# A decoder chain on one Trainium2 core: the norm after cross attention begun earlier, and its turn put inside the matmuls ahead of it

## The reference

```python
# layer 0 (decoder block), after its causal self attention
x = x + cross_attention(ln2(x), ctx) @ out_w + out_b          # 16 heads of 16
x = x + gelu(ln3(x) @ mlp1_w + mlp1_b) @ mlp2_w + mlp2_b
# layer 1: routing attention over the context, gates u and r, candidate, layernorm
# layer 2, after its self attention
x = x + cross_attention(ln2(x), ctx) @ ca_wo + ca_bo          # 16 heads of 64
a, g = split(ln3(x) @ ff_w1 + ff_b1)
x = x + (a * gelu(g)) @ ff_w2 + ff_b2
# layer 3
x = layernorm(cross_attention8(x, ctx) @ Wo + x) * gamma + beta
```

## Time and profile before

| | |
|---|---|
| median of 3 runs | 2139.35 us (2139.18 to 2140.95) |
| profiled execution, its own time | 2139.63 us |
| its span | 2137.7 us, so 1.9 us lie around it |
| PE busy | 2017.7 us (94%) |
| DVE, ACT, POOL busy | 1127.9, 937.1, 749.0 us |
| mean granted PE clock | 0.981 of full |

### The profile page before, as it was taken

How to read it: one execution, slowest core, us unless ns; L and a number is a source line. 1 busy time by engine, 2 the same in 40 slices (tenths; PEclk the granted TensorE clock), 3 DMA queues, 4 the chain that set the end, 5 groups by cost and what they waited for, 6 DMA issues and landing times. The chain is left out here.

```text
span 2137.7 us, 26706 instructions
## 1 busy us (share of the span) xinstructions
PE 2017.7 (94%) x10334; PEld 1200.1 (56%) x10334; DVE 1127.9 (53%) x2009; ACT 937.1 (44%) x1449; POOL 749.0 (35%) x563
## 2 busy tenths in 40 slices
PE   5989998899998999999999999999999999999997
PEld 3544444677676854444544445444543868677776
DVE  4677772534545357756555555555454243546453
ACT  3356666333434425554355554555356431222221
POOL 1222212021212126657566664666464010212121
PEclk9999999999999979999999999999999999999999
DMA  7734332000000021100000000000000430000000
GB/s 147 137 36 52 43 57 85 1 1 1 1 1 1 1 67 39 32 1 1 1 1 1 1 1 1 1 1 1 1 1 1 113 97 1 1 11 3 7 10 10
DMA packets 48044, 51.81 MB, mean 24 GB/s; under 512 B 14682, under 2 KB 38940, under 8 KB 47620
## 3 DMA queue, kind: packets, MB, share of 16 engines
q1 hardware_dynamic: 47924, 50.19, 11.3%
HBM read 41.24 MB, written 8.80 MB: 23 GB/s over the span
## 5 line engine op out<-in xcount | busy, mean ns | idle before, releaser
L1992 POOL TENSOR_TENSOR total<-total,pr 128x1024 f32<-128x1024 f32 x183 | 444.4, 2428 | 232.4 <-ACT pr L2202 215.6
L2202 ACT ACTIVATE pr<-sc 128x1024 f32<-128x1024 f32 x256 | 260.1, 1023 | 266.6 <-PE sc L1868 262.1
L2013 DVE TENSOR_REDUCE pmax<-ring 128x1 f32<-128x512 f32 x512 | 314.5, 684 | 98.2 <-PE ring L1816 98.2
L1868 PE MATMUL sc<-q_full,k_full 64*128 64x512 f32 x1024 | 295.0, 589 | 0.0
L1886 PE MATMUL o<-pr,v_pair 128*64 128x512 f32 x1024 | 247.7, 605 | 0.0
L1816 PE MATMUL ring<-k_round,q_round 64*128 64x512 f32 x512 | 214.2, 569 | 5.8 <-DVE k_round L2007 2.0
L645 ACT ACTIVATE probs<-s 128x512 f32<-128x512 f32 (+1 forms) x304 | 154.8, 579 | 95.7 <-PE s L360 94.9
L483 DVE TENSOR_REDUCE row_max<-s 128x1 f32<-128x1024 f32 (+3 forms) x128 | 125.0, 1019 | 59.2 <-PE s L346 58.9
L1816 PEld LDWEIGHTS ring<-k_round,q_round 64*128 64x128 f32 x512 | 78.7, 190 | 137.3 <-DVE pmax L2013 115.2
L1868 PEld LDWEIGHTS sc<-q_full,k_full 64*128 64x128 f32 x1024 | 129.0, 191 | 26.1 <-issue 16.8
L1886 PEld LDWEIGHTS o<-pr,v_pair 128*64 128x64 f32 x1024 | 62.2, 136 | 138.7 <-issue 121.6
(11 more groups left out here) (362 smaller groups left out, 3438.5 us busy)
## 6 DMA issues: line engine op xcount, KB each, us to landing
qk_dram<-qk_parts SPq DMA_DIRECT2D x32, 192.0 KB, 2.7
q_stack<-qk_dram SPq DMA_DIRECT2D x48, 128.0 KB
k_stack<-qk_dram SPq DMA_DIRECT2D x48, 128.0 KB
x<-in_x SPq DMA_DIRECT2D x4, 512.0 KB, 7.4
region<-in_L_xattn_mlp_w SPq DMA_DIRECT2D x2, 1024.0 KB, 7.9
region<-in_L_xattn_ff_w SPq DMA_DIRECT2D x1, 2048.0 KB, 18.8
out<-region SPq DMA_DIRECT2D x8, 256.0 KB, 2.2
region<-in_L_xattn_sa_wo SPq DMA_DIRECT2D x1, 1024.0 KB, 8.0
```

The lines of the kernel that those rows point to most:

```text
L1868: ins = te.matmul(s2[at % 2][:, j], kf[n % 2][head[j], keys], qf[n % 2][head[j], halves[half]], start=False, stop=True)
L1992: pool.tensor_tensor(out=total[half][:], in0=other[:], in1=probs[at % KEPT][:], op=ALU.add).then_inc(sums, 1)
L2013: dve.tensor_reduce(part_max[:, j, t, half:half + 1], ring[bank_of_max(i)][:], AX.X, ALU.max).then_inc(s1_free, 1)
L2202: act.activation(probs[here % KEPT][:], s2[at % 2][:], ACT.Exp).then_inc(s2_free, 1)
```

## The change

In the first chain, DVE's order in `cross` is written anew: stream 0's add, statistics and moments come between stream 1's reciprocals and stream 1's multiply `vT`; stream 0's normalise comes behind that multiply; then stream 1 follows. PE does the turn of stream 0's norm between the two tiles of stream 1's projection, where it was behind both. In the second chain, PE does the turn of stream 0's norm between chunks 4 and 5 of the eight in stream 1's last values. And in the last block of the second chain DVE finishes stream 0 altogether (norm, scaling) before it adds stream 1's last result.

```diff
-def cross_tensor(te, ch, e, name, i, vw, cols, out_bias):
+def cross_tensor(te, ch, e, name, i, vw, cols, out_bias, between=None):
...
         for c in range(cols // P):
+            if between is not None and s + t == 2 and c == cols // P // 2:
+                between()
...
                         ins = add_bias(te, ch, dst, 0)
+                        if s == 1 and t == 0:
+                            turn_step(te, ch, e, i, "n3", 0)
                     ins.then_inc(ch.te[s].sem, ch.te[s].one("ca.out"))
...
                 cross(i, first)
-                turn_step(te, ch, e, i, "n3", 0)
...
+                def moments(s):
+                    add_vector(dve, ch, e, "ca.x", i, "ca.out", s, bank=1, x=own(s, i))
+                    norm_vector(dve, ch, "n3", i, lambda s: own(s, i), lambda s: after_spare(dve, ch, s, "ca.x", i),
+                                scaled=True, streams=[s])
...
+                inverse(0)
+                divided(0)
+                inverse(1)
+                moments(0)
+                divided(1)
+                normed(0)
+                moments(1)
+                normed(1)
...
                 cross(i)
-                for s in range(B):
-                    add_vector(dve, ch, e, "ca.x", i, "ca.out", s, bank=1, x=own(s, i))
-                    norm_vector(dve, ch, "n3", i, x, lambda s: after_spare(dve, ch, s, "ca.x", i), streams=[s])
...
-                cross_tensor(te, ch, e, "cb", i, e.vw2, 1024, 0)
-                turn_step(te, ch, e, i, "n9", 0)
+                cross_tensor(te, ch, e, "cb", i, e.vw2, 1024, 0, lambda: turn_step(te, ch, e, i, "n9", 0))
...
                         tail.dve[s].sem, tail.dve[s].one("x.last"))
-                if last:
-                    finish_block(i, True)
+                    if last:
+                        finish_block(i, True, [s])
```

More of the change, by code:

```diff
@@ L771, in norm_gpsimd, with scaled_vector @@
             ch.pool[s].sem, ch.pool[s].one(f"{name}.rstd"))
-def scaled_vector(dve, ch, name, i, source, gain, bias, dst, done):
-    for s in range(B):
+def scaled_vector(dve, ch, name, i, source, gain, bias, dst, done, streams=range(B)):
+    for s in streams:
         after(dve, ch.pool[s], f"{name}.rstd", i)
@@ L1388, in cross, with inverse @@
                                           op=ALU.subtract).then_inc(*one(s, f"less{t}"))
-                for s in range(B):
+                def inverse(s):
                     after(dve, ch.act[s], "ca.exp1", i)
@@ L1395, in cross, with divided @@
                     dve.reciprocal(ch.total[s][:], ch.total[s][:]).then_inc(*one(s, "inverse"))
+                def divided(s):
                     after(dve, ch.act[s], "ca.raw", i)
@@ L1399, in cross, with normed @@
                                       in1=caT[s][:].rearrange("p g t -> p (g t)"), op=ALU.mult).then_inc(*one(s, "vT"))
+                def moments(s):
+                    add_vector(dve, ch, e, "ca.x", i, "ca.out", s, bank=1, x=own(s, i))
+                    norm_vector(dve, ch, "n3", i, lambda s: own(s, i), lambda s: after_spare(dve, ch, s, "ca.x", i),
+                                scaled=True, streams=[s])
+                def normed(s):
+                    after(dve, ch.pool[s], "n3.rstd", i)
+                    for t in range(2):
+                        ins = dve.tensor_scalar(ch.h[s][:, t, :], own(s, i)[:, t, :], ch.moments[s][:, t, 0:1],
+                                                ch.rstd[s][:, t:t + 1], ALU.subtract, ALU.mult)
+                    ins.then_inc(ch.dve[s].sem, ch.dve[s].one("n3.h"))
+                inverse(0)
[6 more added lines that the diff above has]
+                normed(1)
             def finish_block(i):
@@ L2582, in head, with finish_block @@
                     ins.then_inc(*one("h", s))
-            def finish_block(i, waits):
+            def finish_block(i, waits, streams=range(B)):
                 last = lambda s: ch.xc[s][:]
-                norm_vector(dve, tail, "n10", i, last, lambda s: after_spare(dve, tail, s, "x.last", i), scaled=True)
+                norm_vector(dve, tail, "n10", i, last, lambda s: after_spare(dve, tail, s, "x.last", i), scaled=True,
+                            streams=streams)
                 if waits:
-                    for s in range(B):
+                    for s in streams:
                         dve.wait_ge(stored[s], 16 * i)
-                scaled_vector(dve, tail, "n10", i, last, w.vec["gamma"], w.vec["beta"], lambda s: result[s], "out")
+                scaled_vector(dve, tail, "n10", i, last, w.vec["gamma"], w.vec["beta"], lambda s: result[s], "out",
+                              streams)
             def emit(i, first, last):
```

## The result

The changed kernel took 2125.39 us (median of 4 runs, 2123.96 to 2127.10) against 2139.70 us (4 runs): a ratio of 0.9932 (95% interval 0.992 to 0.9944), 14.3 us less. Five more runs of it, against other runs of the kernel before, gave 0.9951 (0.9938 to 0.9963) and a median of 2129.24 (e6); over all nine the median is 2127.10, where 2127.0 had been forecast. The spread, from 2121.06 to 2131.33, is two and a half times that of the kernel before (2138.27 to 2142.44 over all its runs), and e6 and e10 are about it. The profiled execution took 2123.96 us, its span 2122.0.

What follows compares the result with a forecast made beforehand. PE, busy 94% of the span, was taken to bound the kernel, gains coming only where it waits. 9.33 + 3.76 + 0.58 - 1.3 = 12.4 us off 2139.35 us gave 2127.0 us; range 2123.6 to 2131.8.

Steps and rivals of the forecast that it cites:

- First chain, 9.33 us: First chain, four blocks: stream 0's add starts when the reciprocals end, so the MLP starts earlier; 9.33 us saved.
- The first block: First chain's first block: stream 0's projection ends late, MLP at 408.76 in place of 410.82; 2.06 us saved.
- The widening beside DVE, 0 us: First chain: POOL's widening of stream 1 beside DVE's add and statistics costs nothing; bounds 0 and 3.0 us.
- rival 3: First chain: DVE and POOL hold each other up, `vT` late by the whole widening; 2129.9 to 2133.7 us; chance 0.08.
- Second chain, 3.76 us: Second chain, four blocks: stream 0's turn inside stream 1's last values lets the feed-forward start without a wait; 3.76 us saved.
- The new wait: Second chain, stream 1's turn: PE waits about 0.5 us for stream 1's `h`, taking 0.48 us of the gain.
- The end, 0.58 us: End of the second chain: stream 0 finished first, stream 1 added 1.71 us later; 0.58 us saved.
- The clock, -1.3 us: First chain: two clock falls at 1.5 us against 1.69 us paid now; -1.3 us, bounds +1.7 and -5.1 us.
- forecast's own sign: First chain: the forecast is wrong if, among other signs, the clock falls more than twice.
- Rival 2: First chain: the clock falls in every block, now in the open; 8.6 us saved, 2130.8 us; chance 0.13.
- Rival 4: First chain gains nothing, paced by something other than PE further on; 4.3 us saved elsewhere, 2135 us; chance 0.03.
- rival 5: First chain: slower, as `vT` of stream 1 waits behind stream 0's add, late by 4.5 us a block; chance 0.04.

Runs made afterwards that it cites:

- e6: The changed kernel run again without an edit, against the kernel before: 2129.24 us, ratio 0.9951.
- e10: Changed kernel with unused identity turns filling PE's two gaps ahead of stream 1's projection in the first chain: 2120.11 us, ratio 0.9911 to the kernel before.
- e12: The kernel before with unused identity turns filling the same PE gaps as in e10: 2138.63 us, ratio 0.9993.
- e8: e7's kernel with another end, stream 0's second scaling behind stream 1's add: 2121.49 us, ratio 0.9915 to the kernel before.
- e2: Changed kernel with the first chain and the end put back, leaving only the second chain's change: 2136.92 us, ratio 0.9987 to the kernel before.
- e7: Changed kernel with stream 1's turn in the second chain four PE instructions later: 2123.84 us, ratio 0.9922 to the kernel before.
- e3: Only the end changed, stream 0 finished ahead of stream 1's last add: 2140.18 us, ratio 1.000 to the kernel before.
- e1: Changed kernel with the second chain's turn and the end put back, leaving only the first chain's change: 2126.67 us, ratio 0.9937 to the kernel before.
- e9: Changed kernel with stream 0's turn in the second chain two chunks earlier: 2128.46 us, ratio 0.9942 to the kernel before.
- e4: Only DVE's new order in the first chain, PE's turn behind both tiles, the rest put back: 2131.72 us, ratio 0.9962 to the kernel before.
- e5: Only PE's turn between the first chain's projection tiles, DVE's order and the rest put back: 2138.93 us, ratio 0.9994 to the kernel before.

## Why the prediction was right

The gaps were read rightly, and they make most of the gain. The term of the clock was not read rightly, and it came out well by luck.

- **First chain, 9.33 us.** Shown. In the first profile the four blocks save 1.98, 2.53, 2.37 and 2.54 us up to the MLP (the first block taken from the start of stream 0's projection, the others from stream 1's), 9.42 us; 0.17 us each of the second's and the fourth's is a fall that was almost hidden before. The four distances that the sum was made of held within 0.05 us: from the add's start to the aggregate's end 1.71 us (493.13 to 494.84), to `h` 2.81 us, to the turn 3.60 us, and from the turn to the MLP 1.77 us. The 0.06 us for a late `vT` is not there. The 0.05 us at stream 1's turn is: the next matmuls start 0.48 us behind that turn's start, before 0.43 us.
- **The first block** was forecast with two errors of reading. From the turn to its MLP are 1.86 us before and after, and not 1.77. And stream 0's projection was late there behind a fall of the clock (granted 0.57 from 396 to 400 us): in e10 and e12, without that fall, stream 1's projection starts 4.81 us behind stream 0's in both, and the block saves 2.37 us like the others. The bias put at 594.18 us adds up to 594.07; nothing hangs on it.
- **The sum of the first chain without the clock** can be estimated from e12 and e10. In e12, 395.56 us less its two falls at 1.69 us is 392.18. In e10, stream 0's first projection starts 41.54 us behind the chain's start, in e8 without a fall 40.40, so 384.01 less 1.14 is 382.87. The difference is 9.3 us, as forecast.
- **The widening beside DVE, 0 us.** Shown: 0.74 us, and statistics of 0.42 us, as without a neighbour. The bound of 3.0 us was not needed; rival 3 is out.
- **Second chain, 3.76 us.** 3.56 us in e2. Up to stream 1's turn the blocks of the first profile save 1.00, 0.87, 0.87 and 0.98 us, 3.7 in all; most of the rest is that a turn for which PE has waited holds it 0.49 us and not 0.44. The new wait is there. Its four rows add up to 1.1 us, but the turn starts 3.95 us behind the feed-forward (1857.01 to 1860.96), whose 16 matmuls hold PE for 3.46 us, so 0.49 us are lost in this block, as forecast (0.38 in the first and the last); e7 gets back 1.97 us by moving that turn.
- **The end, 0.58 us.** 0.51 us measured (e3). e8 shows that its cause was named rightly: stream 1's add stood behind stream 0's scaling, 1.8 us.
- **The clock, -1.3 us.** A fall in the open was priced rightly: 1.5 us taken, 1.56 measured in e6. What was paid before was not. The forecast counted one fall at 1.69 us, in the third block. The profile of before has two more ahead of the first block's projection, one of them at the chain's start:

```profile
358.49 1.92 PE L1102 MATMUL c_ps<-ident,region 128*128 128x128 f32 x8 [1.08 <-PEq L74]
```

By the estimate above the clock cost 3.85 us in the first chain before (396.03 less 392.18), and after 1.35 us in the first profile, 4.63 in e6 and 8.27 in e1. So the term was +2.5 us, -0.8 us and -4.4 us in three executions. By the forecast's own sign (more than two falls in the first chain) it failed in e1 and in e6 to e9. And the falls outside the first chain (2.7 and 1.7 us) were not counted at all. They may be more than luck: the four profiles with the old first chain (before, e2, e3, e12) have both of them, and of the ten others only the first one of the changed kernel has. Nothing here shows why.
- **Rival 2** (a fall in every block) did happen in the first chain of e1 and e9, and in all blocks behind the first in e6, e7 and e8, so its 0.13 was low. Its price was near: 4.2 us left of the first chain (9.33 less 5.1), 4.9 measured in e1. The total stayed below its 2130.8 us in most runs, and in e1's and e9's profiles the self attention and the start of the second chain were 4.2 us shorter. Rival 4 is out, since the part from the MLP to the next projection is 87.53 us before and 87.57 after; rival 5 too. The lower end of the range, 2123.6, is 0.4 us below what its own sum gives (2139.35 less 15.36).

What was luck: the two profiled executions lie 15.7 us apart, 3.3 more than the 12.4 forecast. The clock in the first chain makes about +3.8 us of this (+2.5 in place of -1.3) and the second chain with the end -0.3. The 14.3 us in the first four runs and 2127.1 as the median of all nine both lie near the forecast, but either could have come out 2 us away with the same kernel.

## What to carry to other kernels

When an engine idles between two streams' steps, look at what stands next in its list for the other stream: here 1.7 us of add and statistics fitted into DVE's wait of 1.6 us for a widening and a turn. Move the consumer's instruction as well: e4 and e5 show that DVE's order alone is worth two thirds of it and PE's place alone nothing. And after closing a gap, ask for the next late one: moving stream 1's turn by four instructions, and not putting stream 0's last scaling ahead of stream 1's add, gave another 4 us that the change had left.

## What was not expected of the hardware

A PE gap can cost more than itself. In e6 the granted clock fell to half, in three blocks, behind stretches in which PE had been working with gaps of 0.85 to 1.1 us, and each fall cost 1.56 us. It doesn't fall each time: the first profile has the same gaps and no fall in these blocks. 1.5 us of useless turns in such gaps gave a faster kernel (0.9911, interval 0.9897 to 0.9924, clear of e6's 0.9951 and barely touching the 0.9932 of the first runs). And a fall can be hidden: in the kernel before it cost 1.7 us in the MLP, and 0.2 us at a projection behind which PE had to wait anyway (5.45 us against 5.28). The same kernel took from 2121.06 to 2131.33 us, so a difference of one or two us between two such kernels is read from the parts of their traces and not from a few times.
